# Norms of q and k as four 64x64 products, squares crossed by DMA, q, k and exponentials left in PSUM

## What is computed

```python
qkv = x @ Wqkv; q, k, v = split(qkv, 3)          # 16 heads of 64
q = l2norm(q) * qs;  k = l2norm(k) * ksc          # t / max(norm over the 64 features, 1e-12)
q = q * cos * scale + rotate_half(q) * sin * scale
k = k * cos / scale + rotate_half(k) * sin / scale
sim = einsum('bhwie,bhwje->bhwij', bq, look(bk)) * 8.0   # a window sees itself and the one before
attn = softmax(where(mask, -max, sim));  out = attn @ look(bv)
x = x + out @ Wo;  x = x + ffn(x)                 # ffn: layer norm, W1, a * gelu(gate), W2
```

## Time and profile before

| | us |
|---|---|
| median of 2 runs | 2688.89 (2684.29 to 2693.5) |
| the profiled execution, its own time | 2695.59 |
| its span | 2693.8 |
| granted clock of TensorE, mean | 0.962 |

### The profile page before, as it was taken

One profiled execution on the slowest core, in us unless ns is written; L12 is line 12 of the kernel. 1 busy time (PEld: TensorE's weight loads), 2 busy tenths in 40 slices (PEclk: granted clock), 3 DMA queues, 4 the chain that ended last, 5 costly groups with the idle time before them and its releaser, 6 DMA issues. The chain is left out here.

```text
span 2693.8 us, 62735 instructions
## 1 busy us (share of the span) xinstructions
PE 2427.3 (90%) x24940; PEld 1267.8 (47%) x24940; DVE 2276.3 (85%) x2595; ACT 1801.3 (67%) x2593; POOL 1082.1 (40%) x461
## 2 busy tenths in 40 slices
PE   7899999999999999999999999999999977767778
PEld 2355555445555555455555555455545522222355
DVE  5799998998899998999889988998889848999542
ACT  4667776777677766777667766677677656545533
POOL 0344444444444444444444444444444303556130
PEclk8899999999999999999999999999999989999989
DMA  0100000000000000000000000000000010000001
GB/s 20 53 2 2 2 25 10 10 2 1 14 22 10 2 2 13 14 18 1 2 14 14 15 5 2 13 14 9 10 2 2 2 36 0 0 0 0 18 16 47
DMA packets 16016, 29.85 MB, mean 11 GB/s; under 512 B 3616, under 2 KB 6064, under 8 KB 15664
## 3 DMA queue, kind: packets, MB, share of 16 engines
q1 hardware_dynamic: 15760, 25.78, 3.1%
HBM read 24.73 MB, written 1.05 MB: 10 GB/s over the span
## 5 line engine op out<-in xcount | busy, mean ns | idle before, releaser
L707 POOL TENSOR_TENSOR f_rot<-f_raw,f_tabc 128x1024 f32<-128x1024 f32 x192 | 453.8, 2364 | 993.6 <-DVE f_qk L755 448.6
L711 POOL TENSOR_TENSOR f_rot<-f_rot,f_shuf 128x1024 f32<-128x1024 f32 x192 | 452.0, 2354 | 235.5 <-DVE f_shuf L748 235.5
L606 ACT ACTIVATE f_raw<-f_ps 128x1024 f32<-128x1024 f32 x192 | 196.1, 1021 | 348.6 <-PE f_ps L430 348.6
L748 DVE TENSOR_TENSOR f_shuf<-f_shuf,f_tabs 128x1024 f32<-128x1024 f32 x192 | 417.9, 2177 | 8.7
L778 DVE TENSOR_TENSOR f_s<-f_s,f_rcp 128x512 f32<-128x512 f32 x192 | 401.0, 2089 | 6.6
L477 PEld LDWEIGHTS f_ps<-f_ptz,f_v 64*64 64x64 f32 x6144 | 259.5, 133 | 96.0 <-issue 96.0
L477 PE MATMUL f_ps<-f_ptz,f_v 64*64 64x96 f32 (+1 forms) x6144 | 285.9, 243 | 1.9 <-ACT f_ptz L627 1.7
L429 PE MATMUL f_ps<-f_xs,f_wq 128*128 128x512 f32 x384 | 225.2, 670 | 46.9 <-DVE f_xs L726 34.6
L745 DVE STREAM_SHUFFLE f_shuf<-f_raw 128x1024 f32<-128x1024 f32 x192 | 257.7, 1342 | 0.6
L755 DVE SCALAR_TENSOR_TENSOR f_qk<-f_rn,f_rot 128x1024 f32<-128x1024 f32 x192 | 233.0, 1214 | 2.5 <-POOL f_rot L711 2.5
L456 PE MATMUL f_ps<-f_qk 64*32 64x64 f32 x12288 | 198.8, 220 | 34.8 <-issue 34.8
(11 more groups left out here) (267 smaller groups left out, 3894.9 us busy)
## 6 DMA issues: line engine op xcount, KB each, us to landing
e_w<-in_e_w SPq DMA_DIRECT2D x16, 256.0 KB, 2.8
f_wq<-in_f_wq SPq DMA_DIRECT2D x12, 256.0 KB, 2.8
f_wk<-in_f_wk SPq DMA_DIRECT2D x12, 256.0 KB, 3.5
f_wv<-in_f_wv SPq DMA_DIRECT2D x12, 256.0 KB, 3.5
f_wo<-in_f_wo SPq DMA_DIRECT2D x6, 512.0 KB, 3.4
f_w<-in_f_w SPq DMA_DIRECT2D x6, 341.0 KB, 2.9
s_dx<-in_k_pick SPq DMA_DIRECT2D x1, 1536.0 KB, 9.0
f_w<-in_f_w SPq DMA_DIRECT2D x6, 192.0 KB, 3.3
```

What stands on the lines that cost most here:

```text
L707: pool.tensor_tensor(view(rot, 0, [S, 4], [1, S]), view(raw, 0, [S, 4], [1, S]), view(tab_c, 0, [S, 2], [0, 2], [1, S]), ALU.mult).then_in ...
L711: pool.tensor_tensor(rot[:, :], rot[:, :], shuf[:, :], ALU.add).then_inc(sem["rot"], 1)
L748: dve.tensor_tensor(view(shuf, 0, [S, 4], [1, S]), view(shuf, 0, [S, 4], [1, S]), view(tab_s, 0, [S, 2], [0, 2], [1, S]), ALU.mult).then_i ...
```

## The change

- The weights of q and k are rearranged on the host so that the first projection gives q of one head on partitions 0 to 63 and k of the other head on 64 to 127, and the second projection the reverse. The tables and scales follow, and `qk` gets other offsets.
- `raw` and its copy are gone. ACT squares straight from banks 0 and 1 (`square`), DVE shuffles from there and does the cosine product itself (`straight`, into `rot`), POOL does the sine product and then the sum (`rotate`).
- `norms` becomes four products of 64 rows by 64 columns: two on `sq`, two on `cross`, which holds the squares' other halves moved to the other 64 partitions. They write banks 6 and 7. `cross` is filled by two DMAs of 128 KB per unit, issued by SP once `sq` is there (`swap`); the weight loads stand between the swaps.
- The values move to bank 6, the transposes to bank 2. The exponential is written to banks 4 and 5, and the sums and the product of `soft_b` read it there.
- New waits: `project` for the squares, the shuffle and the cosine product of the unit before; `norms` for `cross`, for the values' copy and for the output's copy; `scores` for the product of `soft_b` of the unit before; `mix` for the Ln.
- Order: on ACT the exponential comes ahead of the squares. On DVE `soft_b` comes ahead of the shuffle and the cosine product. In slot 5 `hid_mm` 0 comes ahead of `gate_mm` 0, which now waits for the Ln.

```diff
+        def swap(sp, t, q):
+            gather(sp, sem["sq"], t + q + 1)
+            sp.dma_start(cross[64:128, :], sq[0:64, UNIT:]).then_inc(sem["cross"], 16)
+            sp.dma_start(cross[0:64, :], sq[64:128, 0:UNIT]).then_inc(sem["cross"], 16)
...
             def project(i, j):
-                need(pe, sem["ln"], i * 8 + j)
+                need(pe, sem["sq"], i * 8 + j)
+                need(pe, sem["shuf"], i * 8 + j)
+                need(pe, sem["straight"], i * 8 + j)
...
             def norms(i, j):
-                need(pe, sem["sq"], i * 8 + j + 1)
-                pe.matmul(bank(0), same_head[:, :], sq[:, 0:UNIT], start=True, stop=True)
-                pe.matmul(bank(1), same_head[:, :], sq[:, UNIT:], start=True, stop=True).then_inc(sem["n_mm"], 1)
+                gather(sem["sq"], i * 8 + j + 1)
+                gather(sem["cross"], i * 256 + 32 * j + 32)
+                gather(sem["v"], i * 8 + j + 1)
+                gather(sem["o"], i * 8 + j - 3)
+                for own in (True, False):
+                    for h in range(2):
+                        k = slice(64 * h, 64 * h + 64)
+                        of = sq[k, UNIT * h:UNIT * h + UNIT] if own else cross[k, :]
+                        mm = pe.matmul(view(ps, NBANK[h] * CH, [1, CH], p0=64 * (h if own else 1 - h), rows=64),
+                                       same_head[k, k], of, start=True, stop=True, skip_group_check=True)
+                mm.then_inc(sem["n_mm"], 1)
...
             def scores(i, j):
-                gather(sem["shift"], i * 8 + j)
+                gather(sem["p"], i * 8 + j)
...
-            def raw_copy(i, j):
+            def square(i, j):
                 need(act, sem["a_mm"], i * 8 + j + 1)
-                act.activation(view(raw, 0, [UNIT, 2], [1, UNIT]), bank(0, 2), ACT.Copy).then_inc(sem["raw"], 1)
                 need(act, sem["n_mm"], i * 8 + j)
-                act.activation(sq[:, :], raw[:, :], ACT.Square).then_inc(sem["sq"], 1)
+                act.activation(view(sq, 0, [UNIT, 2], [1, UNIT]), bank(0, 2), ACT.Square).then_inc(sem["sq"], 1)
...
         @block.gpsimd
-            def straight(i, j):
-                need(pool, sem["raw"], i * 8 + j + 1)
-                need(pool, sem["qk"], i * 8 + j)
-                pool.tensor_tensor(view(rot, 0, [S, 4], [1, S]), view(raw, 0, [S, 4], [1, S]),
-                                   view(tab_c, 0, [S, 2], [0, 2], [1, S]), ALU.mult).then_inc(sem["straight"], 1)
+            def rotate(i, j):
+                need(pool, sem["shuf"], i * 8 + j + 1)
+                pool.tensor_tensor(view(shuf, 0, [S, 4], [1, S]), view(shuf, 0, [S, 4], [1, S]),
+                                   view(tab_s, 0, [S, 2], [0, 2], [1, S]), ALU.mult).then_inc(sem["turned"], 1)
                 need(pool, sem["straight"], i * 8 + j + 1)
                 need(pool, sem["turned"], i * 8 + j + 1)
                 pool.tensor_tensor(rot[:, :], rot[:, :], shuf[:, :], ALU.add).then_inc(sem["rot"], 1)
...
         @block.vector
+            def straight(i, j):
+                need(dve, sem["sq"], i * 8 + j + 1)
+                need(dve, sem["qk"], i * 8 + j)
+                dve.tensor_tensor(view(rot, 0, [S, 4], [1, S]), view(ps, 0, [S, 4], [1, S]),
+                                  view(tab_c, 0, [S, 2], [0, 2], [1, S]), ALU.mult).then_inc(sem["straight"], 1)
...
-                if has:
-                    rotate(u, a)
                 if before and j == 6:
                     hidden(k, 1)
                 if run:
                     soft_b(i, j)
+                if has:
+                    shuffle(u, a)
+                    straight(u, a)
```

More of the change, by code:

```diff
@@ L367, in local_attention, with gather @@
         n_const = 16 * len(consts)
[L369 to L377, removed]
+        def gather(sp, sm_, value):
+            if not isinstance(value, int) or value > 0:
+                sp.wait_ge(sm_, value)
+                sp.sem_inc(sem["listed"], 1)
@@ new lines, in layer @@
+        def layer(sp, r, first, last):
+            for q in range(8 * NU):
+                swap(sp, r * 8 * NU, q)
+                if not first and q == 4:
+                    load_wo(sp, r, r * NU)
+                if not first and q == 9:
+                    load_w1(sp, r, r * NU)
+                if not first and q == 10:
+                    load_w2(sp, r, r * NU)
+                if not last and q == 8 * NU - 5:
+                    load_qkv(sp, r + 1, (r + 1) * NU, 0)
+                if not last and q == 8 * NU - 1:
+                    load_qkv(sp, r + 1, (r + 1) * NU, 1)
@@ L392, in _ @@
             load(sp, sem["const"], consts)
-            weights(sp, 0, 0)
-            with sp.Fori(1, DEPTH) as r:
-                weights(sp, r, r * NU)
+            for k in range(2):
+                load_qkv(sp, 0, 0, k)
+            load_wo(sp, 0, 0)
+            load_w1(sp, 0, 0)
+            load_w2(sp, 0, 0)
+            layer(sp, 0, True, False)
+            with sp.Fori(1, DEPTH - 1) as r:
+                layer(sp, r, False, False)
+            layer(sp, DEPTH - 1, False, True)
         @block.tensor
@@ L652, in slot @@
                     nc.scalar.preload_act_table_set(ACT_SET)
+                if run:
+                    need(act, sem["shift"], i * 8 + j + 1)
+                    act.activation(view(ps, 4 * CH, [CH, 2], [64, 4], [1, 64]), view(s[j % 2], 0, [64, 2], [128, 4], [1, 64]),
+                                   ACT.Exp, scale=8.0).then_inc(sem["exp"], 1)
                 if has:
-                    raw_copy(u, a)
+                    square(u, a)
                 if before and j == 4:
@@ L657, in slot @@
                     act.activation(sq2[:, :], cen[:, :], ACT.Square).then_inc(sem["sq2"], 1)
-                if has and j == 5:
-                    value_copy(u, a)
-                if run:
-                    need(act, sem["shift"], i * 8 + j + 1)
-                    act.activation(s[j % 2][:, :], s[j % 2][:, :], ACT.Exp, scale=8.0).then_inc(sem["exp"], 1)
-                if has and j != 5:
+                if has:
                     value_copy(u, a)
@@ L842, in _ @@
             for t in qk:
[L843 removed]
+                for at in AT:
+                    mm = dve.memset(t[:, at - WIN:at], 0.0)
             mm.then_inc(sem["zero"], 1)
```

117 lines of the change are left out of this document (68 added, 49 removed).

## The result

| | before | after |
|---|---|---|
| median of 2 runs, us | 2688.89 | 2795.15 (2792.94 to 2797.37) |
| ratio, with its 95% interval | | 1.0391 (1.0353 to 1.0430) |
| span of the profiled execution, us | 2693.8 | 2791.1 |
| granted clock, mean | 0.962 | 0.954 |

What follows compares the result with a forecast made beforehand. PE was taken to set the pace before; with the change, slots sum to 89.1 us against 87.7, plus 2.7 of half clock: 4.1 more per iteration, 90 us over 22 and about 4 unrolled, giving 2788 us, range 2675 to 2900.

Steps and rivals of the forecast that it cites:

- The norms: Four 64x64 products on PE at 1.0 us, 0.72 less per unit, 138 us over 192 units if PE stays the bound.
- The rival in which PE stays the bound: Swap under 1.5 us and no more half clock: 2555 us, or 2620 with chain A binding in slots 3 to 5; chance 0.14.
- The swap: Squares reach PE through SP and two 128 KB transfers: 2.6 us, bounds 2.0 and 3.3, where before 0.1 us.
- Slots 2 to 4: 9.9 us by Chain B; 10.1 by chain A plus 1.0 for held `shift_in`; 9.5 by Chain B, variance and slot 3's delay.
- Chain B: From `scores` to `scores` through projections, squares, swap and norms: 8.1 us, plus work ahead of projections or behind norms.
- chain A: Loop of shuffle, POOL's two operations, `normalise`, `soft_b`, next shuffle: 9.05 us, and no slot can be shorter.
- The sign that was named for it: `normalise` should wait for POOL's sum in slots 3 and 4.
- Slot 5: 12.4 us: L825 waits for the variance's Ln and Exp, delaying exponential, squares, swap and norms; the worst chain.
- Slots 6 and 7: 11.2 and 11.7 us, sums along scores, projections, squares, swap, norms, with gates and mix, or values and W2.
- Slot 0: 14.5 us: 15.2 of before less 0.7 for the norms, keeping the loop's hole and half clock.
- The clock's step: A 3.1 us PE hole in slot 5 brings one more half-clock stretch: 2.7 us per iteration, bounds nothing and 13.
- likeliest band of 2750 to 2830: The forecast's own case, 2750 to 2830 us; chance 0.40.

Runs made afterwards that it cites:

- e1_tiles: Kernel before with only the norms changed to four 64x64 products on the squares where they lie, no swap, some norms to the wrong head: 2666 us, ratio 0.9915.
- e2_noswap: Changed kernel without the two transfers per unit; the second pair of norms products reads squares on their own partitions, so norms of wrong heads: 2663 us, ratio 0.9891.
- e7_pool: Changed kernel without the swap, variance ahead of the norms, and POOL's sum of the rotation cut to 16 columns: 2500 us, ratio 0.9276.
- e4_sqfirst: Changed kernel with the squares ahead of the exponential on ACT, the order of before: 2747 us, ratio 1.0197.
- e3_var: Changed kernel with the variance product ahead of the norms in slot 4, and its Ln and Exp ahead of the unit's on ACT: 2691 us, ratio 0.9992.
- e11_bvar: Kernel before with the variance product ahead of its norms in slot 4 and its logarithm ahead of theirs on ACT: 2708 us, ratio 1.0040.
- e5_late: Changed kernel with the norms one slot later, variance at the end of slot 4, all three gate products in slot 6: 2842 us, ratio 1.0544.
- e10_late2: Changed kernel with the norms one slot later, variance at the end of slot 4, gate 0 kept in slot 5: 2838 us, ratio 1.0533.
- e12_shift: Changed kernel without swap, early variance, four tiles from where squares lie; ACT's logarithm carries k's norms across partitions; computes the whole: 2595 us, ratio 0.9629.

## Why the prediction was right, step by step

**The norms** were taken at 1.0 us and measured 1.02. That the four tiles do run together holds. "138 us, if PE stays the bound" did not come, and e1_tiles shows that even alone it would have been 28: the condition was not true of the kernel before in five slots of eight. The rival in which PE stays the bound (2555 or 2620) could not come in: with a swap that costs nothing (e2_noswap) the changed kernel takes 2663. At 0.14 it had too much.

**The swap** is the term that was mis-sized: 2.6 us taken, 3.3 the upper bound, 3.4 measured. ScalarE and SyncE in slot 5:

```profile
961.40 1.01 ACT L656 ACTIVATE f_sq<-f_ps 128x1024 f32<-128x1024 f32 x1
...
962.50 0.46 SPq L401 DMA_DIRECT2D f_cross<-f_sq  x1
963.00 0.60 SPq L402 DMA_DIRECT2D f_cross<-f_sq  x1
```
```profile
f_cross<-f_sq SPq DMA_DIRECT2D x384, 128.0 KB, 2.3
```

The squares end at 962.41 and the norms start at 965.80: 3.39 us, and 3.38 to 3.50 in the other five slots of this iteration where they wait. The parts: 0.1 us to SP, 0.5 until the second issue, 2.4 to the second transfer's landing (965.4; the first took 2.2), and 0.4 from there to PE's start. The forecast had 0.1, 0.42 and 2.1 for the first three and nothing for the last: half of the 0.8 is the way from the landing to PE, the rest is mostly the landing. The Trainium skill, DMA: Bandwidth & Descriptors, section Anatomy of one DMA, gives by its figures an estimate of 2.6 for another path; here 2.9 passed from the first issue to the second landing (962.50 to 965.4), 0.3 above it.

**Slots 2 to 4**: 9.9, 10.1 and 9.5 forecast, 10.5, 9.8 and 9.7 measured. Chain B with a swap of 3.4 gives slot 2 10.7, near its 10.5. The floor of chain A was worked out as 9.05; on DVE and POOL it reads:

```profile
943.07 1.30 DVE L791 STREAM_SHUFFLE f_shuf<-f_ps 128x1024 f32<-128x1024 f32 x1
...
945.38 1.44 DVE L871 TENSOR_SCALAR f_fcol<-f_cols 128x9 f32 x1
...
949.34 1.23 DVE L805 SCALAR_TENSOR_TENSOR f_qk<-f_rn,f_rot 128x1024 f32<-128x1024 f32 x1
951.44 0.69 DVE L830 TENSOR_TENSOR f_s<-f_ps,f_rcp 128x512 f32<-128x512 f32 x1
...
952.05 1.29 DVE L791 STREAM_SHUFFLE f_shuf<-f_ps 128x1024 f32<-128x1024 f32 x1
```

8.98 us from shuffle to shuffle, with POOL's two operations between (944.44 to 949.31). e7_pool shows it as a bound by shortening it, in a kernel without the swap. In after it binds neither slot 3 nor slot 4. The sign that was named for it, `normalise` waiting for POOL's sum there, didn't come: it waited 11 times in 1000 us, in slot 0, by 0.5 us.

```profile
L805 DVE SCALAR_TENSOR_TENSOR f_qk<-f_rn,f_rot 128x1024 f32<-128x1024 f32 x89 | 108.3, 1216 | 7.0 <-POOL f_rot L757 5.6
```

Slot 3 was forecast as A's, and is B's, entered late: squares at S+5.4, swap 3.4, norms 1.0, with S the start of its scores. `shift_in` is held by POOL (L772 1.32 us, 0.29 before, twice; L770 1.35, 0.42 before), 3.0 us in sum where the forecast took 1.0; it delays `soft_a`, that the exponential, and behind that stand the squares; e4_sqfirst, which takes the squares out from behind it, brings slot 3 to 8.7. So the 10.1 forecast for slot 3 is near the 9.8 measured by another road than the one that it was worked out on.

**Slot 5** went nearly as worked out, with S the start of its scores: L878, the successor of L825, was to start at S+2.65 and did at S+2.64, the squares were to end at S+6.7 and did at S+6.2, the norms start at S+9.3 and did at S+9.6 (squares 0.5 early, swap 0.8 long).

```profile
958.81 0.69 DVE L878 TENSOR_TENSOR f_xn<-f_cen,f_sq 128x512 f32<-128x512 f32 x1 [4.35 <-ACT f_sq L725]
```

With its half clock it was to be 15.1 and is 14.2 in the mean. e3_var settles that this is one wait: an exchange gives the slot back (10.9 for 10.8 before). The chain by which the variance's logarithm stands behind the norms', which stand behind the swap, is with the swap's own 132 us the costliest thing in the changed kernel, though the diff does not touch the variance's place in the order.

**Slots 6 and 7**: 11.2 and 11.7 forecast, 12.2 and 13.5 measured. The swap's 0.8 is in both. Of slot 7 another 1.0 is left; it has stretches at half clock in some iterations (in the one before the one shown, values that start at 893.48 take 1.98 us), 17 us in the 22, which is worth up to 0.4 us each. The other part lies behind the norms: from their start to the next scores 4.3 us pass in the mean, where 3.6 was taken.

**Slot 0** is the large miss: 14.5 forecast, 10.1 measured. The working kept the loop's hole of 1.49 us and the half clock behind it; in after there is a hole of 0.58 here (0.83 at most) and no half clock in this iteration (its window reads 1.00), and 2 us of it in 22 iterations. That gave 3.8 us back where 0.7 was forecast, and covered what slots 6, 7 and 2 took too much. The clock's step was right in kind: one stretch in slot 5, of 1.6 us not 2.7, but it is in place of the one in slot 0, not beside it. In the loop 78.5 us ran at half clock before, 100.5 after. Why the hole is gone is open. It stands inside the scores at every turn of the loop in the three kernels with the old order of work (before, e1_tiles, e11_bvar: 1.7, 2.4 and 1.8 us in the mean), and in none of the others. Most of those have one ahead of the scores instead, 0.4 to 0.9 us in the mean; in e5_late and e10_late2 it is 1.4 us, and there slot 0 has 72 and 120 us at half clock again.

**The sum**: 4.1 us per iteration forecast, 3.4 measured, and 22 us outside the loop where 4 were. (The iteration read for the base, 87.7 us, is 1.3 above the mean of 22.) The forecast's time is right to 0.3%, and its likeliest band of 2750 to 2830 holds the result, but in part by luck, by errors that met: slot 0 was 4.4 us too long, slots 2, 6 and 7 together 3.4 too short, each about as much as the sum itself. That the change costs time rested on the swap's chain, and this held.

## What to carry to other kernels

Before costing a saving, ask of each stage what would bind next: in e1_tiles 0.7 us off every unit was worth 0.15. A short operation that is moved behind a transfer takes with it everything that its engine issues afterwards, so look for work of other chains queued behind the new wait, and move that ahead first. Where data must cross partitions, look whether an engine that reads it anyway can write it there: e12_shift did for 0.75 us of ScalarE what two transfers did in 3.4 us, of which PE stood idle for 1.5 to 3.4 in six slots of eight.

## What the runs showed of the hardware

- Copies with a single input, SBUF to SBUF, are held by POOL's work on VectorE: the 9 columns of `fcol` took 0.16 us before and take 1.44 when they meet L753 (L871 starts at 945.38 and ends at 946.82, POOL's operation started at 944.44 and took 2.35), and 64x255 took 0.29 and takes 1.32. The prediction said that no row showed this; the Trainium skill, SBUF — State Buffer, section Who interferes with whom, states it of `tensor_scalar`, and these rows agree.
- ScalarE reads PSUM on 64 partitions and writes SBUF on the other 64 at the price of a straight pass (0.59 us for 512 columns).
- Four 64x64 tiles run at once, with two of them writing each bank. In after the two that share a bank read the same 64 rows; in e12_shift they read different rows (0 to 63 and 64 to 127) and write partitions 0 to 63 and 64 to 127 of the bank. It costs nothing extra: the norms take 1.03 us from their start (945.33) to the next scores (946.36), against 1.02 in after. Four tiles in four banks were not tried.

```profile
945.33 1.09 PE L480 MATMUL f_ps<-f_sq,f_same 64*64 64x512 f32 x8 [0.62 <-ACT f_o L683]
946.36 0.39 PE L495 MATMUL f_ps<-f_maskb,f_identb 128*128 128x256 bf16 x2
```
